# Sharing one 256-column matmul between early and late queries of a key block, in a causal attention kernel

## The chip, the core and the metric
The kernel runs on one core of a Trainium2 chip. The metric is the device time of one execution in microseconds. The core's engines are TensorE (PE, with its weight loads shown apart as PEld), VectorE (DVE), ScalarE (ACT), GpSimd (POOL) and SyncE (SP), which here only issues DMAs. Each runs its own instruction stream in order; semaphores tie them together.

## What is computed
For 64 batches of 128 tokens and 512 features, with 16 heads of 64, one shared key and value head, a learned bias, a null key and a causal mask:

```python
B, N, DIM, H, DH = (64, 128, 512, 16, 64)
xn = layernorm(x, g_in)
q = (xn @ Wq).reshape(b, n, H, DH).transpose(0, 2, 1, 3) * DH ** -0.5
kv = xn @ Wkv
k, v = kv[..., :DH], kv[..., DH:]           # then nk, nv are put in front
sim = einsum('bhid,bjd->bhij', q, k) + bias  # key 0 is the null key
sim = where(causal or masked out, -max, sim)
out = einsum('bhij,bjd->bhid', softmax(sim), v)
out = out.transpose(0, 2, 1, 3).reshape(b, n, H * DH) @ Wo
return x + layernorm(out, g_out)
```

Everything is float32. The projections (`project`, `project_out`) split each operand into a high and a low part of type fp32r and run three matmuls for one product; the scores and the product of weights and values use plain f32, for which the trace shows two weight loads and two matmul records for each call in the code.

## The kernel before
Work is tiled by batch. Two batches make a group (`GB`), two groups a pair, and `run_pairs` unrolls the first and the last of 16 pairs and loops over those between. Within a pair there are `CP` = 16 steps t, four for each batch; one step is four heads of one batch: two head pairs u, each in one half of the 128 partitions, and two heads e. Queries are split in halves: a *late* query (64 to 127) needs 128 keys, an *early* one (0 to 63) only the first 64. So a step holds 2 x 128 late logits (`BOT`) and 2 x 64 early ones (`TOP`) in each partition.

One step goes like this. PE makes the scores of two steps at once (`scores`, L387), at even t. DVE adds bias and mask and finds the largest (`logits`, L492). ACT takes the exponentials and their sums (`exponentials`, L679): late ones, then early ones. DVE inverts the sums (L501). POOL normalizes into `w_nrm` (L799, one instruction for the late, one for the early part). DVE transposes the 384 columns in blocks of 32 x 32 into `wt` (L508), which therefore has 12 blocks for each batch, 8 late and 4 early, each with 4 steps x 32 queries = 128 columns. Partition rows 32g to 32g+31 of `wt` hold the queries' block with u = g // 2 and h = g % 2, where h says which 32 of the 64 queries of a half.

Once a batch, after its four steps, PE multiplies weights and values (`values`, L411): for each g, each head e and each key block j that the queries of that block need, one call with 32 rows, 64 columns of values as weights and the 128 columns of one block of `wt` as moving data. It writes into `ps_pv[g]`, whose 256 columns are step c, late or early l, query q. h = 0 needs late blocks 0, 1, 2 and early block 0; h = 1 needs late 0 to 3 and early 0, 1. With u and e that is 16 + 24 = 40 calls. `ITEMS` is that list, and the loop takes rank r of it on all of g before the next rank. A pair (g, e) is one 32 x 64 tile of the PE array; there are eight.

Then ACT adds the null value and makes the high part (`heads_hi`, L687, four instructions, one for each g), DVE the low part (`heads_lo`, L513, four), and PE multiplies with Wo (`project_out`, L424, 24 matmuls of 512 columns). `project_out` waits for `o_lo_made` to be two, i.e. for the second of the four `heads_lo`, and after 12 matmuls for the fourth. It writes into the bank of `ps_pv[0]`. Layernorm, residual and store follow.

The order on each engine is written out by hand. On PE a step is: scores if t is even, `values` if due, parts of the next projections (`front`: x transposes L448, kv and q projections L430, 12 matmuls for each part) and `project_out` if due. By `PLAN`, `values` and the `heads` of a batch are due in the same even step and `project_out` in the one after. The first batch of a group has `values` at t % 8 = 6, followed by one q part of 12 matmuls; the second has it at t % 8 = 2, followed by the kv part of 12 matmuls. On ACT an even step is: late exponentials, the four `heads_hi`, early exponentials. On DVE it is: logits of two steps, the four `heads_lo`, then copies of q (L568) and transposes.

Of the kernel before, what the change touches and what calls it, by code (L numbers as in the profile page):

```python
# [12 lines left out]
B, N, DIM = 64, 128, 512  # L13
H, DH = 16, 64
# [14 lines left out]
HALF = N // 2  # L29
BLK = 32  # L30
BOT, TOP = 2 * N, 2 * HALF
# [33 lines left out]
STEP_STATS, STEP_XN, STEP_V, STEP_MASK = 4, 7, 7, 7  # L65


ITEMS = (
    [(1, 0), (1, 1), (1, 2), (0, 0)],
    [(1, 0), (1, 1), (1, 2), (1, 3), (0, 0), (0, 1)],  # L70
)


def attention_block(nc, x, attn_bias, null_kv, mask, g_in, null_bias, wq, wkv, wo, g_out, out):
# [4 lines left out]
    with ExitStack() as ctx:  # L79
        def sb(name, shape, dt=F32):  # L80
            return ctx.enter_context(nc.sbuf_tensor(name, shape, dt))

        def psum(name, shape):
            return ctx.enter_context(nc.psum_tensor(name, shape, F32))

        def sem(name):
            return ctx.enter_context(nc.semaphore(name))
# [43 lines left out]
        v32 = sb("v32", [P, 2, GB, N // BLK, DH])  # L131
# [8 lines left out]
        exp_bot, exp_top = sb("exp_bot", [P, 2, 2, N + 1]), sb("exp_top", [P, 2, 2, HALF + 1])  # L140
        w_sum = sb("w_sum", [P, 2, HC])
        w_inv = sb("w_inv", [P, 2, HC])
        w_nrm = sb("w_nrm", [P, 2, BOT + TOP])

        wt = sb("wt", [P, 2, WBLOCKS, CB, BLK])
# [15 lines left out]
        ps_pv = [psum(f"ps_pv{g}", [P, DIM]) for g in range(4)]  # L161
# [36 lines left out]
        pv_done, o_hi_made, o_lo_made = sem("pv_done"), sem("o_hi_made"), sem("o_lo_made")  # L198
# [18 lines left out]
        def wait(eng, s, value):  # L217

            if isinstance(value, int) and value <= 0:
                return  # L220
            eng.wait_ge(s, value)  # L221

        def apart(eng):

            eng.sem_inc(waits_taken, 1)  # L225
# [6 lines left out]

        def bot_top(row):
            return row[:, 0:BOT].rearrange("p (e n) -> p e n", e=2), row[:, BOT:].rearrange("p (e n) -> p e n", e=2)

        def steps(last):
            return range(CP + (TAIL if last else 0))
# [11 lines left out]
        def of_tile(ps):  # L249

            return ps[:, 0:2 * N].rearrange("p (c l q) -> p c l q", c=CB, l=2)
# [13 lines left out]
        block = ctx.enter_context(nc.Block())  # L265
# [105 lines left out]
        def _(pe):  # L371
# [22 lines left out]
            def values(p, batch, back):  # L394

                slot, b = back // GB % 2, back % GB
                wait(pe, wt_made, CB * batch + CB)
                wait(pe, o_lo_made, 4 * batch)
                wait(pe, y_nrm_made, batch)
                if back % GB == 0:  # L400
                    wait(pe, v_made, 2 * p + back // GB + 1)
                apart(pe)
                for r in range(len(ITEMS[1])):
                    for g in range(4):
                        if r >= len(ITEMS[g % 2]):
                            continue
                        late, j = ITEMS[g % 2][r]
                        rows = slice(BLK * g, BLK * (g + 1))
                        for e in range(2):
                            block = N // BLK * e + j if late else 2 * (N // BLK) + HALF // BLK * e + j  # L410
                            mm = pe.matmul(of_tile(ps_pv[g])[DH * e:DH * (e + 1), :, late], v32[rows, slot, b, j],  # L411
                                           wt[rows, b, block],
                                           start=(r == 0), stop=(r == len(ITEMS[g % 2]) - 1))
                            if r == len(ITEMS[g % 2]) - 1:
                                mm.then_inc(pv_done, 1)

            def project_out(batch):
                todo = [(o, w, 2 * c + u) for u in range(2) for c in range(CB)
# [45 lines left out]
            def body(p, first, last):  # L464
                for t in steps(last):
                    if t % 2 == 0 and t < CP:
                        scores(p, t)
                    for batch, back in due("pv", p, t, first, last):
                        values(p, batch, back)
                    for f, slot, kind, i in front_parts(p, t, first, last):  # L470
                        front(f, slot, kind, i)
                    if first and t == PLAN["out"]:
                        pe.wait_ge(wo_lo_by_dve, WP // 2)
                        pe.wait_ge(wo_lo_by_pool, WP // 2)
                    for batch, back in due("out", p, t, first, last):
                        project_out(batch)
# [4 lines left out]
        def _(dve):  # L481
            def logits(n, t):
                s = t % 2
                wait(dve, bias_b_made, n + 1)
                wait(dve, s_done, 2 * (n - s) + 4)
                wait(dve, exp_made, n - 1)
                apart(dve)
                for i, (bias, out_) in enumerate(zip(bot_top(bias_b[:, s]), (logit_bot[:, s], logit_top[:, s]))):
                    keys_ = bias.shape[2]
                    for e in range(2):  # L490
                        from_ = WIDE * s + N * i
                        ins = nc.vector.tensor_tensor_reduce(  # L492
                            out_[:, e, 0:keys_], ps_s[e][:, from_:from_ + keys_], bias[:, e], -1.0, 0.0,
                            ALU.add, ALU.min, neg_max[:, s, 2 * i + e:2 * i + e + 1])
                    ins.then_inc(s_read, 1)
# [285 lines left out]
        def _(pool):  # L781
            def masked_bias(n, g, t):
                slot, b, c, s = t // CG % 2, t // CB % GB, t % CB, t % 2
                if t % CG == 0:
                    wait(pool, mask_made, g + 1)
                wait(pool, s_read, 2 * (n - 1))
                for out_, bias in zip(bot_top(bias_b[:, s]), bot_top(bias_c[:, c])):
                    keys_ = out_.shape[2]
                    key_mask = mask_add[:, slot, b, 0:keys_].unsqueeze(1).to_broadcast([P, 2, keys_])
                    ins = nc.gpsimd.tensor_tensor(out_, bias, key_mask, ALU.add)  # L790
                ins.then_inc(bias_b_made, 1)

            def normalize(n, t):
                s = t % 2
                wait(pool, inv_made, n + 1)
                wait(pool, wt_made, n - 1)
                for i, (out_, w_exp) in enumerate(zip(bot_top(w_nrm[:, s]), (exp_bot, exp_top))):
                    keys_ = out_.shape[2]
                    ins = nc.gpsimd.tensor_tensor(out_, w_exp[:, s, :, 0:keys_],  # L799
                                                  w_inv[:, s, 2 * i:2 * i + 2].unsqueeze(2).to_broadcast([P, 2, keys_]),  # L800
                                                  ALU.mult)
                ins.then_inc(nrm_made, 1)
# [72 lines left out]
            def body(p, first, last):  # L875
                for t in steps(last):
                    n = CP * p + t
                    for done in due("norm", p, t, first, last):
                        y_scale(*done)
                    if t % 2 == 0 and t < CP - 2 * last:  # L880
                        for ahead in range(2, 4):
                            masked_bias(n + ahead, 2 * p + (t + ahead) // CG, (t + ahead) % CP)
                    if t < CP:
                        normalize(n, t)
                    if not last and t % CG == STEP_STATS + 1:
                        x_rstd_of(2 * p + t // CG + 2)
                    if first and t == PLAN["add"]:
                        pool.wait_ge(ld_gout, 16)
                    for done in due("add", p, t, first, last):
                        residual(*done)  # L890
                    if first and t in first_extras:
                        first_extras[t]()
# [25 lines left out]
```

## Time and profile before

| | |
|---|---|
| Time, median of three runs | 1152.41 us (1152.06, 1152.41, 1154.45) |
| Span of the profiled execution | 1154.5 us |
| PE matmul busy | 1061.4 us, 92% |
| PE weight load busy | 923.9 us, 80% |
| POOL / DVE / ACT busy | 804.2 us, 70% / 729.0 us, 63% / 674.2 us, 58% |
| Matmul records of L411 (weights x values) | 5120, 107.3 us busy |
| Matmul records of L430, xt_hi x wq_hi alone | 1024, 298.5 us busy |

The span of the profiled execution is within 0.1 us of the highest of the three times, so nothing of note lies around the span. Busy times of PE overlap each other, since the matmuls of different tiles of the array run side by side and their ends are modelled. "Busy" alone does not say that an engine sets the end; for that the chain of waits and the order in time have to be read.

### The profile page before, as it was taken

The numbers are of one execution on the slowest core, as the hardware profiler recorded it, in microseconds if no ns is written. First come the engines' busy times: TensorE is split into PE (matmuls) and PEld (weight loads), VectorE is DVE, ScalarE is ACT, GpSimd is POOL, SyncE is SP. The second block draws the span as 40 slices with busy tenths as digits, with TensorE's granted clock in tenths as the row PEclk, the third lists the DMA queues.
The fourth block names the chain that finished last, engine by engine and source line by source line (L and its number), as shares of the span: only waits on it lengthen the run. The fifth ranks groups of instructions, "written<-read, shape, count | busy, mean of one in ns | idle before, by whom it ended". The sixth has DMA issues, their size and how long they took to land.

```text
span 1154.5 us, 43028 instructions
## 1 busy us (share of the span) xinstructions
PE 1061.4 (92%) x14464; PEld 923.9 (80%) x14464; DVE 729.0 (63%) x3536; ACT 674.2 (58%) x2666; POOL 804.2 (70%) x1488
## 2 busy tenths in 40 slices
PE   4799999999999999999999999999999999999975
PEld 4678888888888888888888888888888888888864
DVE  4757666656666666766765766755766665666551
ACT  3656556566556556556655655656655656655651
POOL 2657777667777667777767777767777766777763
PEclk9999999999999999999999999999999999999987
DMA  8211211211221211220221121121121121121011
GB/s 224 64 40 49 67 57 40 66 61 45 68 65 31 67 60 47 66 67 31 65 66 44 65 66 41 55 66 56 50 68 51 45 67 58 48 66 47 30 39 36
DMA packets 51548, 67.72 MB, mean 59 GB/s; under 512 B 13888, under 2 KB 25664, under 8 KB 51392
## 3 DMA queue, kind: packets, MB, share of 16 engines
q1 hardware_dynamic: 49280, 63.21, 17.6%
q8 instruction: 138, 2.26, 0.8%
q10 hardware_dynamic: 2112, 2.10, 0.6%
q14 instruction: 18, 0.15, 0.0%
HBM read 40.11 MB, written 16.78 MB: 49 GB/s over the span
## 4 chain that ended last, share of the span: by engine, by line
PE 77%; ACT 8%; issue 6%; DVE 4%; POOL 1%; ACTq 0%; DVEq 0%; POOLq 0%
PE ps_pv L424 33%; PE ps_proj L430 32%; PE ps_s L387 7%; PE ps_pv L411 4%; ACT exp_bot L679 3%; ACT exp_top L679 2%; DVE o_lo L513 2%; ACT xt_hi L710 1%; DVE logit_bot L492 1%; PE ps_proj L448 1%; ACT o_hi L687 1%; ACTq L221 0%; DVEq L221 0%; DVE y_stats L521 0%; DVEq L225 0%
## 5 line engine op out<-in xcount | busy, mean ns | idle before, releaser
L679 ACT ACTIVATE exp_bot<-logit_bot,neg_max 128x129 f32<-128x129 f32 x512 | 201.7, 397 | 342.3 <-DVE neg_max L492 336.9
L430 PE MATMUL ps_proj<-xt_hi,wq_hi 128*128 128x256 f32 x1024 | 298.5, 292 | 4.1 <-DVE q_sb L568 3.9
L790 POOL TENSOR_TENSOR bias_b<-bias_c,mask_add 128x256 f32<-128x256 f32 (+1 forms) x512 | 289.6, 598 | 1.6 <-DVE neg_max L492 0.3
L492 DVE CUSTOM_DVE_ANT_0 logit_bot<-ps_s,bias_b 128x128 f32<-128x128 f32 x512 | 128.7, 289 | 255.4 <-PE ps_s L387 226.8
L430 PE MATMUL ps_proj<-xt_lo,wq_hi 128*128 128x256 f32 x1024 | 288.0, 281 | 0.0
L430 PE MATMUL ps_proj<-xt_hi,wq_lo 128*128 128x256 f32 x1024 | 287.9, 281 | 0.0
L424 PE MATMUL ps_pv<-wo_hi,o_hi 128*128 128x512 f32 x512 | 211.8, 414 | 51.1 <-DVE o_lo L513 51.1
L799 POOL TENSOR_TENSOR w_nrm<-exp_bot,w_inv 128x256 f32<-128x256 f32 x256 | 156.6, 612 | 120.0 <-DVE w_inv L501 118.8
L424 PE MATMUL ps_pv<-wo_lo,o_hi 128*128 128x512 f32 x512 | 204.9, 400 | 0.0
L424 PE MATMUL ps_pv<-wo_hi,o_lo 128*128 128x512 f32 x512 | 204.8, 400 | 0.0
L430 PEld LDWEIGHTS ps_proj<-xt_hi,wq_hi 128*128 128x128 f32 x1024 | 192.8, 188 | 14.3 <-issue 5.1
L430 PEld LDWEIGHTS ps_proj<-xt_hi,wq_lo 128*128 128x128 f32 x1024 | 193.0, 188 | 0.0
L430 PEld LDWEIGHTS ps_proj<-xt_lo,wq_hi 128*128 128x128 f32 x1024 | 192.9, 188 | 0.0
L679 ACT ACTIVATE exp_top<-logit_top,neg_max 128x65 f32<-128x65 f32 x512 | 172.8, 343 | 0.0
L424 PEld LDWEIGHTS ps_pv<-wo_hi,o_hi 128*128 128x128 f32 x512 | 97.7, 191 | 82.9 <-DVE o_lo L513 55.3
L508 DVE STREAM_TRANSPOSE wt<-w_nrm 128x384 f32<-128x384 f32 x256 | 131.4, 551 | 0.0
L387 PEld LDWEIGHTS ps_s<-keys,q_sb 64*64 64x64 f32 x4096 | 97.6, 133 | 39.9 <-issue 35.7
L821 POOL TENSOR_TENSOR small<-y_mv,small 128x1 f32<-128x1 f32 x64 | 12.1, 190 | 167.6 <-DVE y_mv L527 167.6
L387 PE MATMUL ps_s<-keys,q_sb 64*64 64x128 f32 (+1 forms) x4096 | 114.9, 250 | 7.2 <-DVE neg_max L492 3.7
L513 DVE SCALAR_TENSOR_TENSOR o_lo<-ps_pv,small,o_hi 128x256 fp32r<-128x256 f32 x256 | 106.2, 477 | 21.8 <-ACT o_hi L687 21.8
L424 PEld LDWEIGHTS ps_pv<-wo_hi,o_lo 128*128 128x128 f32 x512 | 97.7, 191 | 23.8
L424 PEld LDWEIGHTS ps_pv<-wo_lo,o_hi 128*128 128x128 f32 x512 | 97.9, 191 | 21.0
(61 smaller groups left out, 1850.7 us busy)
## 6 DMA issues: line engine op xcount, KB each, us to landing
x_in<-in_x_dram SPq DMA_DIRECT2D x32, 512.0 KB, 4.1
x_res<-in_x_dram SPq DMA_DIRECT2D x64, 256.0 KB, 2.8
out_dram<-y_out SPq DMA_DIRECT2D x64, 256.0 KB, 2.0
v_rep<-v_raw SPq DMA_DIRECT2D x256, 32.0 KB, 1.9
w_raw<-in_L_cond_Wq_dram ACTq DMA_DIRECT2D x4, 512.0 KB, 7.9
w_raw<-in_L_cond_Wo_dram SPq DMA_DIRECT2D x4, 512.0 KB, 6.1
mask_u<-in_mask_BxS_bk_dram SPq DMA_DIRECT2D x32, 32.0 KB, 3.7
bias_c<-in_fside_16xSxS_dram SPq DMA_DIRECT2D x4, 128.0 KB, 8.1
```

The source lines that it names most:

```text
L387: mm = pe.matmul(scored[HALF * u:HALF * (u + 1)], q_sb[rows, slot, t % CB + s, u, from_:from_ + HALF], keys[rows, slot, b, 0:N if late els ...
L411: mm = pe.matmul(of_tile(ps_pv[g])[DH * e:DH * (e + 1), :, late], v32[rows, slot, b, j], wt[rows, b, block], start=(r == 0), stop=(r == le ...
L424: mm = pe.matmul(ps_o[:], o[:, i % 2, i // 2], w[:, i], start=(j == 0), stop=(j == len(todo) - 1))
L430: mm = pe.matmul(ps[:, 0:TOK], w[:, k, cols], xt[:, k], start=(j == 0), stop=(j == len(todo) - 1))
L448: mm = pe.transpose(ps[:, N * j:N * (j + 1)], xn[:, b, P * k:P * (k + 1)], ident[:])
L492: ins = nc.vector.tensor_tensor_reduce(out_[:, e, 0:keys_], ps_s[e][:, from_:from_ + keys_], bias[:, e], -1.0, 0.0, ALU.add, ALU.min, neg_ ...
L508: nc.vector.transpose(wt[:, par, :, c], w_nrm[:, s]).then_inc(wt_made, 1)
L513: nc.vector.scalar_tensor_tensor(out=place_of(o_lo, g), in0=of_tile(ps_pv[g]), scalar=nv_col[:, 0:1], in1=place_of(o_hi, g).bitcast(F32), ...
L679: ins = nc.scalar.activation(out_[:, s, j], in_[:, s, j], ACT.Exp, bias=neg_max[:, s, k:k + 1], scale=-1.0, accum_out=w_sum[:, s, k:k + 1])
L790: ins = nc.gpsimd.tensor_tensor(out_, bias, key_mask, ALU.add)
L799: ins = nc.gpsimd.tensor_tensor(out_, w_exp[:, s, :, 0:keys_], w_inv[:, s, 2 * i:2 * i + 2].unsqueeze(2).to_broadcast([P, 2, keys_]), ALU. ...
L821: nc.gpsimd.tensor_tensor(y_var[:, c], y_mv[:, b, 1:2], eps_col[:, 0:1], ALU.add).then_inc(y_var_made, 1)
```

## The change
The list of calls in `values` becomes `VISITS`. Where both the late and the early queries of a (g, e) need key block j, one call takes the early and the late block of `wt` together, 256 columns, and writes both halves of `ps_pv[g]`. This holds for j = 0 with both h and for j = 1 with h = 1: 12 calls of 256 columns in place of 24 of 128. The 16 others keep their 128 columns. The total is 28 calls; the columns are the same 5120 for each batch. So that the early block comes first and the two blocks are a constant step apart, POOL writes the early part of `w_nrm` to the front (`top_first`) and the late one behind it; its instructions stay in the same order and size. No semaphore, wait or buffer changes.

```diff
-ITEMS = (
-    [(1, 0), (1, 1), (1, 2), (0, 0)],
-    [(1, 0), (1, 1), (1, 2), (1, 3), (0, 0), (0, 1)],
-)
+TOP_BLOCKS = TOP // BLK
+VISITS = [
+    [(0, 0, 2), (1, 0, 2)],
+    [(1, 1, 2), (0, 1, 1)],
+    [(0, 2, 1)],
+    [(1, 2, 1)],
+    [(1, 3, 1)],
+]
+KEY_BLOCKS = (3, 4)
...
+        def top_first(row):
+            return row[:, TOP:].rearrange("p (e n) -> p e n", e=2), row[:, 0:TOP].rearrange("p (e n) -> p e n", e=2)
...
-                for r in range(len(ITEMS[1])):
-                    for g in range(4):
-                        if r >= len(ITEMS[g % 2]):
-                            continue
-                        late, j = ITEMS[g % 2][r]
-                        rows = slice(BLK * g, BLK * (g + 1))
-                        for e in range(2):
-                            block = N // BLK * e + j if late else 2 * (N // BLK) + HALF // BLK * e + j
-                            mm = pe.matmul(of_tile(ps_pv[g])[DH * e:DH * (e + 1), :, late], v32[rows, slot, b, j],
-                                           wt[rows, b, block],
-                                           start=(r == 0), stop=(r == len(ITEMS[g % 2]) - 1))
-                            if r == len(ITEMS[g % 2]) - 1:
-                                mm.then_inc(pv_done, 1)
+                for visit in VISITS:
+                    for h, j, halves in visit:
+                        for u in range(2):
+                            g = 2 * u + h
+                            rows = slice(BLK * g, BLK * (g + 1))
+                            for e in range(2):
+                                top, bot = HALF // BLK * e + j, TOP_BLOCKS + N // BLK * e + j
+                                blocks = slice(top, bot + 1, bot - top) if halves == 2 else slice(bot, bot + 1)
+                                heads = of_tile(ps_pv[g])[DH * e:DH * (e + 1)].rearrange("p c l q -> p l c q")
+                                mm = pe.matmul(heads[:, 2 - halves:2], v32[rows, slot, b, j], wt[rows, b, blocks],
+                                               start=(j == 0), stop=(j == KEY_BLOCKS[h] - 1))
+                                if j == KEY_BLOCKS[h] - 1:
+                                    mm.then_inc(pv_done, 1)
...
-                for i, (out_, w_exp) in enumerate(zip(bot_top(w_nrm[:, s]), (exp_bot, exp_top))):
+                for i, (out_, w_exp) in enumerate(zip(top_first(w_nrm[:, s]), (exp_bot, exp_top))):
```

## Rows read from the trace of the kernel before

**Rows 1.** Page, parts 1 and 2: busy times; the granted PE clock in 40 slices.
```profile
PE 1061.4 (92%) x14464; PEld 923.9 (80%) x14464; DVE 729.0 (63%) x3536; ACT 674.2 (58%) x2666; POOL 804.2 (70%) x1488
...
PEclk9999999999999999999999999999999999999987
```

**Rows 2.** Page, part 4: the chain that ended last, by engine and by line.
```profile
PE 77%; ACT 8%; issue 6%; DVE 4%; POOL 1%; ACTq 0%; DVEq 0%; POOLq 0%
PE ps_pv L424 33%; PE ps_proj L430 32%; PE ps_s L387 7%; PE ps_pv L411 4%; ACT exp_bot L679 3%; ACT exp_top L679 2%; DVE o_lo L513 2%; ACT xt_hi L710 1%; DVE logit_bot L492 1%; PE ps_proj L448 1%; ACT o_hi L687 1%; ACTq L221 0%; DVEq L221 0%; DVE y_stats L521 0%; DVEq L225 0%
```

**Rows 3.** The chain in order of time, first batch of a group: start, length, what.
```profile
606.41 0.83 PE ps_s L387 x32
607.24 1.57 PE ps_pv L411 x79
608.81 1.61 PE ps_proj L430 x12
610.42 5.79 PE ps_pv L424 x24
```

**Rows 4.** Matmul records of L411 begun by 607.24, by 608.13, by 608.55.
```profile
L411 PE MATMUL ps_pv<-wt,v x8: 318/318/318, 607.2 to 607.2; 32*64 32x128 f32 x8
...
L411 PE MATMUL ps_pv<-wt,v x64: 267/268/318, 607.2 to 608.1; 32*64 32x128 f32 x64
...
L411 PE MATMUL ps_pv<-wt,v x80: 267/268/318, 607.2 to 608.5; 32*64 32x128 f32 x80
```

**Rows 5.** Timeline of PE from 609.9: start, us, engine, line, operation.
```profile
610.02 0.28 PE L430 MATMUL ps_proj<-xt_hi,wq_lo 128*128 128x256 f32 x1
610.14 0.28 PE L430 MATMUL ps_proj<-xt_lo,wq_hi 128*128 128x256 f32 x1
610.33 0.50 PE L424 MATMUL ps_pv<-wo_hi,o_hi 128*128 128x512 f32 x1
610.67 0.40 PE L424 MATMUL ps_pv<-wo_lo,o_hi 128*128 128x512 f32 x1
610.90 0.40 PE L424 MATMUL ps_pv<-wo_hi,o_lo 128*128 128x512 f32 x1
```

**Rows 6.** Second heads_lo and first weight load of L424, first batch, then second.
```profile
609.80 0.47 DVE L513 SCALAR_TENSOR_TENSOR o_lo<-ps_pv,small,o_hi 128x256 fp32r<-128x256 f32 x1
...
610.33 0.19 PEld L424 LDWEIGHTS ps_pv<-wo_hi,o_hi 128*128 128x128 f32 x1
...
627.63 0.47 DVE L513 SCALAR_TENSOR_TENSOR o_lo<-ps_pv,small,o_hi 128x256 fp32r<-128x256 f32 x1
...
628.16 0.19 PEld L424 LDWEIGHTS ps_pv<-wo_hi,o_hi 128*128 128x128 f32 x1 [1.67 <-DVE o_lo L513]
```

**Rows 7.** Timeline of DVE and ACT after the scores of 606.34, first batch.
```profile
607.57 0.29 DVE L492 CUSTOM_DVE_ANT_0 logit_bot<-ps_s,bias_b 128x128 f32<-128x128 f32 x1 [0.39 <-PE ps_s L387]
...
608.12 0.41 ACT L679 ACTIVATE exp_bot<-logit_bot,neg_max 128x129 f32<-128x129 f32 x1 [1.81 <-DVE neg_max L492]
...
608.81 0.19 ACT L679 ACTIVATION_READ_ACCUMULATOR exp_bot<-logit_bot,neg_max 128x1 f32 x1
608.90 0.47 ACT L687 ACTIVATE o_hi<-ps_pv,small 128x256 fp32r<-128x256 f32 x1
```

**Rows 8.** Another first batch, near the end: its L411, and ACT up to heads_hi.
```profile
1088.22 1.64 PE L411 MATMUL ps_pv<-wt,v 32*64 32x128 f32 x80
...
1089.90 0.19 ACT L679 ACTIVATION_READ_ACCUMULATOR exp_bot<-logit_bot,neg_max 128x1 f32 x1
1090.00 0.45 ACT L687 ACTIVATE o_hi<-ps_pv,small 128x256 fp32r<-128x256 f32 x1
```

**Rows 9.** Waits of L687 and for L513 (us, times); last L411 on the chain.
```profile
  PE ps_pv L411: 2.9, 1
...
  PEld ps_pv L424: 55.3, 33
...
1134.59 2.64 PE ps_pv L411 x80
```

## The prediction, made before the changed kernel was run
> **What bounds the kernel now.** I first read the busy times: PE has 92%, no other engine more than 70%, and the granted clock is at its full level (2.4 GHz) until the last slices [rows 1]. So PE is the engine to look at. The chain of waits says the same and gives L411, the line that changes, 4% of the span [rows 2]. Divided by the 1.57 us of one batch's L411 [rows 3] that is 1154.5 x 0.04 / 1.57 = 29 batches of 64: about one of each group of two. For that one, the first batch of a group, the chain goes through PE without a break: scores, weights x values, 12 matmuls of a q part, 24 of L424 [rows 3]. Read that way, each nanosecond that L411 loses in a first batch comes off the end. The second batch of a group is another case: its L424 sits idle for 1.67 us until the second `heads_lo` of DVE (L513) is done [rows 6].
>
> The chain follows a step back to a releaser only where it sees idle time, and matmul ends are modelled. So I ask of the first batch what L424 waits for, too. `project_out` needs the second L513. It ends at 609.80 + 0.47 = 610.27, and the first weight load of L424 starts at 610.33, 0.06 us later; in the second batch it is 627.63 + 0.47 = 628.10 and 628.16, again 0.06 us, and there it certainly waits [rows 6]. PE itself shows a dent at the same place: the q matmuls start 0.12 us apart (610.02, 610.14), so the next would start at 610.26; L424's first record starts at 610.33 and lasts 0.50 instead of 0.40 us, and the second follows 0.34 us later instead of 0.23 [rows 5]. The weight load, which elsewhere runs beside the matmul before it, lies open here. The true start of that matmul is 610.67 - 0.23 = 610.44, so PE lost 610.44 - 610.26 = 0.18 us in waiting. The chain doesn't show it because the modelled end of the last q matmul, 610.14 + 0.28 = 610.42, covers it [rows 5].
>
> What does that L513 hang on? On `heads_hi` of ACT (L687), which needs `pv_done`, the end of L411, and also stands behind the late exponentials on ACT. In this batch ACT reads the last accumulator at 608.81 and begins L687 at 608.90, 0.09 us on, and the row names no wait [rows 7]. The last L411 record had started by 608.55 [rows 4]. Whether L687 followed the one or the other can be told from a batch in which they stand differently. At 1088.22 L411 starts and has the same length of 1.64 us; L687 starts at 1090.00. That is 1.78 us after the start of L411, against 608.90 - 607.17 = 1.73 here (L411's first record is the one of 607.17, 1.64 us long to its modelled end); behind the accumulator read it is 0.10 against 0.09 us [rows 7, 8]. L687 keeps its distance to the exponentials, not to L411. And the wait list has L687 waiting for L411 once in the whole run, 2.9 us, in the last batch [rows 9]. The exponentials in turn wait for the logits, and these for the scores [rows 7], which PE issues ahead of L411. So the path through a first batch is scores, logits (607.57), late exponentials (608.12), `heads_hi` (608.90), `heads_lo`, L424 (610.33). L411 and the 12 q matmuls lie beside it, 0.18 us shorter. In a second batch they are 1.67 us shorter.
>
> **The change part by part.** *Removed:* 12 of 40 calls a batch, that is 24 of 80 matmul records and as many weight loads. *Kept:* all columns. What is it worth within L411? The last 16 records, on the four h = 1 tiles only, are four passes of a tile, and start in 608.55 - 608.12 = 0.43 us: 0.11 us a pass [rows 4]. The 64 before them, eight passes on each of the eight tiles, take 0.95 us, 0.12 us a pass. A pass is bound by its 128 columns, then, and calls for other tiles run beside it; the first eight are all under way by 607.24 [rows 4]. An h = 1 tile has six calls, 12 passes; after the change it has four calls, of which two are wide: four passes of 256 and four of 128 columns, the same 12 units. From the first to the last start it is now 608.54 - 607.17 = 1.37 us [rows 4]. Without any jostling it would be 11 units of 0.109, plus 0.05 for the first (its record is 318 ns, not 268), plus 0.05 until the last tile begins: 1.30 us. So 0.07 us is there to be regained if the lighter stream of calls feeds each tile in time. For the four passes that are merged away on a tile, the fixed cost of a matmul is bounded by L430 and L424: two of 256 columns take 2 x 0.12, one of 512 takes 0.23 [rows 5], which is 0.00 to 0.01 us for each; four give 0.00 to 0.04, and I take 0.02. L411 shrinks by 0.07 + 0.02 = 0.09 us a batch, bounds 0.00 and 0.11.
>
> What of it lies on the path: nothing in first batches, where PE would only reach L424's wait 0.18 + 0.09 us early, and nothing in second ones. That L687 waits for L411 once in the whole run says that this holds at both ends of the kernel, but for the last batch [rows 9]. There, where L411 starts at 1134.59 and ACT idles for it [rows 9], the 0.09 us, or up to twice that at the lower clock of the last slices, comes off: 0.1 us in all.
>
> *New, and not in the trace:* a call whose moving data are two runs of 128 columns and whose output goes to two halves of the bank. Its lower bound is the 0.23 us for 512 columns of L424, so no cost for width; its output now is already runs of 32 columns, with others skipped, and a pass of L411 keeps 0.11 us [rows 4]. I take a wide pass at 2 x 0.109 us. The upper bound is that such a pass runs at half that rate, 0.22 us more for each of four on an h = 1 tile. No row is near that; it makes the slow rival below.
>
> *Moved:* the early part of `w_nrm` goes in front. POOL issues the same two instructions in the same order, DVE the same transpose of 384 columns; only addresses differ: zero, and none of it is a wait. The order of the calls also changes: h = 0 ends after visit 3, h = 1 goes on alone. Even if each of the five visits waited for the one before, L411 would be 2 + 2 + 1 + 1 + 1 = 7 call times of 0.22 where it has 6 now, 0.22 more minus the 0.09 gained: 0.13 us, still within the 0.18 us of slack. What hides this edit is the chain over DVE and ACT; without that cover it would cost 30 x 0.13 = 4 us. No wait is added. Semaphore counts are the same, eight a batch.
>
> The sum against the profiled execution: 1154.5 - 0.1 = 1154.4. That execution lies 0.18% above the median of the three times, 1152.41; the same step from there gives 1152.3.
>
> **The rivals.** *Faster: L411 is on the path of first batches after all.* For it: the chain, read plainly, has L411 in about 29 batches [rows 2, 3]. Against it: the 0.06 us between L513 and L424, equal in a batch that surely waits and in one that is said not to. It gives 29 x 0.09 + 0.1 = 2.7 us: 1149.7. With the upper bound of 0.11 it is 3.3 us: 1149.1. In the same direction goes a rule of the Trainium skill: TensorEngine Tiling (Array Packing), section "Performance Considerations", puts a fixed overhead of about 60 cycles on each matmul, which at 2.4 GHz would be, as an estimate from that page, 25 ns for each of the four passes merged away on a tile, 0.10 us a batch instead of my 0.02. The trace doesn't agree, since two q matmuls of 256 columns take at most 0.01 us more than one matmul of 512 [rows 5], and even so the gain would end in the same wait.
>
> *Slower: wide calls stream at half rate.* Place: the four wide passes of an h = 1 tile. Price: 4 x 0.22 - 0.09 = 0.79 us a batch. It decides once L411 has grown by 0.18 us in first batches, i.e. from some 0.07 us for each wide pass on; second batches forgive 1.67 us. It gives 30 x (0.79 - 0.18) = 18 us, and 1 or 2 us in the last two batches, where the clock is low: 1172. Against it: a call now writes strided runs and shows nothing of it. Half the extra price, 0.39 us, would be 30 x 0.17 = 5 us: 1157.7.
>
> *It doesn't do what it says:* if the 256-column calls are taken apart again, L411 is as now, and so is the time, 1152.4. That lies within the forecast.
>
> **How the numbers follow.** A measurement of this kernel tells about 0.2% from no change, 2.3 us. The likeliest case, with the last one in it, has 0.85: 1152.3, own range 1151.0 to 1153.7 (the three times before lie within 2.4 us of each other, the lower two within 0.4). Faster rival 0.09, slower rival 0.06. The range must leave out no more than 2 in 10; the main case's own range holds nearly all of its 0.85, and I widen it a little toward the faster rival: 1150.4 to 1154.0. Faster by over 0.2%: 0.09, within: 0.85, slower: 0.06.
>
> **What would show it.** In the trace after: 56 records of L411 a batch (3584 in all) over 1.28 to 1.30 us from first to last start, not 1.37; wide passes of about 0.22 us. The first q matmul behind L411 starts 0.09 us earlier relative to it. L424's first weight load still starts 0.06 us after the second L513, and the open time before it grows from 0.18 to about 0.27 us; the chain or the waits may then name DVE L513 in first batches as well. The distance from the first logits to L424 in a first batch stays 610.33 - 607.57 = 2.76 us. I am wrong if L687 moves forward with L411, so that this distance shrinks by 0.09 us (then the faster rival holds), or if L411 grows beyond 1.37 + 0.18 us (then the slower one does).

## The result

The changed kernel is slower. Its median is 1167.2 us in four runs (1166.72 to 1169.43), that of the kernel before 1153.28 us in four; the ratio is 1.0116, with a 95% interval of 1.0095 to 1.0138. The forecast was no change, 1152.3 us, with a range that ended at 1154.0. (The ratios, here and below, are taken from the record, with their intervals; the quotient of two medians differs from them by up to 0.2%.)

The first view is the page of the changed kernel: busy times, the chain by line, and two groups of the q matmuls with the idle time before them.

```profile
PE 1062.6 (91%) x12928; PEld 914.4 (78%) x12928; DVE 730.6 (63%) x3536; ACT 674.6 (58%) x2666; POOL 804.2 (69%) x1488
...
PE ps_pv L432 33%; PE ps_proj L438 31%; PE ps_s L395 7%; PE ps_pv L420 4%; ACT exp_bot L687 3%; ACT exp_top L687 2%; DVE o_lo L521 2%; ACT xt_hi L718 1%; DVE logit_bot L500 1%; ACT o_hi L695 1%; PE ps_proj L456 1%; ACTq L226 0%; DVEq L226 0%; DVE y_stats L529 0%; DVEq L230 0%
...
L438 PE MATMUL ps_proj<-xt_hi,wq_hi 128*128 128x256 f32 x1024 | 298.5, 292 | 14.7 <-issue 10.5
...
L438 PEld LDWEIGHTS ps_proj<-xt_hi,wq_lo 128*128 128x128 f32 x1024 | 193.1, 189 | 11.7 <-issue 11.7
```

Busy times and chain are those of before [rows 1, 2]; 1536 matmul records are gone, as the code says. What is new are 10.5 us ahead of q matmuls and 11.7 us ahead of their weight loads that are put down to "issue": PE waited for nothing that a semaphore shows. The list of waits has the 10.5 us in 13 pieces. This is one of them, from the timeline of PE:

```profile
171.11 0.28 PE L438 MATMUL ps_proj<-xt_lo,wq_hi 128*128 128x256 f32 x1
171.88 0.28 PE L438 MATMUL ps_proj<-xt_hi,wq_hi 128*128 128x256 f32 x1 [0.49 <-issue]
172.00 0.28 PE L438 MATMUL ps_proj<-xt_hi,wq_lo 128*128 128x256 f32 x1
```

In the middle of a run of 24 matmuls that share their waits, one comes 0.77 us after its predecessor instead of 0.12. The same happens near 240.4, 310.0, 379.7 and so on, once in each of 13 passes of PE's loop over pairs, always between the same two matmuls, for 0.5 to 1.4 us. The 13 steps, from one start to the next, sum to 14.2 us, 12.6 us more than 13 x 0.12. The span grew by 1167.6 - 1154.5 = 13.1 us. So nearly the whole loss is there, in code that the change doesn't touch.

The product itself became shorter, by about half of what was forecast. Its records in one first batch, then the time of the whole and the first q matmul behind it:

```profile
L420 PE MATMUL ps_pv<-wt,v x56: 267/289/425, 614.5 to 615.8; 32*64 32x128 f32 x32, 32*64 32x256 f32 x24
...
614.46 1.59 PE L420 MATMUL ps_pv<-wt,v 32*64 32x256 f32 x56
615.98 0.38 PE L438 MATMUL ps_proj<-xt_hi,wq_hi 128*128 128x256 f32 x1
```

From the first record to the q matmul it is 615.98 - 614.46 = 1.52 us; before it was 1.57 [rows 3]: 0.05 us less, where 0.09 was forecast. ACT and PE behind it, in the same batch:

```profile
616.10 0.19 ACT L687 ACTIVATION_READ_ACCUMULATOR exp_bot<-logit_bot,neg_max 128x1 f32 x1
616.19 0.46 ACT L695 ACTIVATE o_hi<-ps_pv,small 128x256 fp32r<-128x256 f32 x1
...
617.08 0.48 DVE L521 SCALAR_TENSOR_TENSOR o_lo<-ps_pv,small,o_hi 128x256 fp32r<-128x256 f32 x1
...
617.61 0.19 PEld L432 LDWEIGHTS ps_pv<-wo_hi,o_hi 128*128 128x128 f32 x1 [0.16 <-DVE o_lo L521]
```

`heads_hi` starts 0.09 us behind the accumulator read as before [rows 7], the first weight load of `project_out` 617.61 - 617.56 = 0.05 us behind the second `heads_lo` [rows 6], and now the profile names that wait in a first batch too. `heads_hi` is 1.73 us behind the product's start (616.19 - 614.46), as it was. From the first logits (614.86) to `project_out` it is 2.75 us, where the prediction had 2.76.

### The profile page after: what moved, and what is told of

Its sections match the earlier page's. It is cut to its first block, busy times and chain, and to the rows that moved or that the text cites. A ratio compares the mean times of both kernels' runs of the same rounds, so it can differ in the third digit from the quotient of the medians.

```text
span 1167.6 us, 39956 instructions
## 1 busy us (share of the span) xinstructions
PE 1062.6 (91%) x12928; PEld 914.4 (78%) x12928; DVE 730.6 (63%) x3536; ACT 674.6 (58%) x2666; POOL 804.2 (69%) x1488
## 4 chain that ended last, share of the span: by engine, by line
PE 76%; ACT 8%; issue 6%; DVE 4%; DVEq 0%; ACTq 0%; POOL 0%; POOLq 0%
PE ps_pv L432 33%; PE ps_proj L438 31%; PE ps_s L395 7%; PE ps_pv L420 4%; ACT exp_bot L687 3%; ACT exp_top L687 2%; DVE o_lo L521 2%; ACT xt_hi L718 1%; DVE logit_bot L500 1%; ACT o_hi L695 1%; PE ps_proj L456 1%; ACTq L226 0%; DVEq L226 0%; DVE y_stats L529 0%; DVEq L230 0%
## 5 line engine op out<-in xcount | busy, mean ns | idle before, releaser
L687 ACT ACTIVATE exp_bot<-logit_bot,neg_max 128x129 f32<-128x129 f32 x512 | 201.5, 397 | 341.7 <-DVE neg_max L500 336.3
L438 PE MATMUL ps_proj<-xt_hi,wq_hi 128*128 128x256 f32 x1024 | 298.5, 292 | 14.7 <-issue 10.5
L438 PEld LDWEIGHTS ps_proj<-xt_hi,wq_hi 128*128 128x128 f32 x1024 | 192.9, 188 | 14.2 <-issue 5.1
L438 PEld LDWEIGHTS ps_proj<-xt_hi,wq_lo 128*128 128x128 f32 x1024 | 193.1, 189 | 11.7 <-issue 11.7
L687 ACT ACTIVATE exp_top<-logit_top,neg_max 128x65 f32<-128x65 f32 x512 | 172.6, 342 | 0.0
L576 DVE COPY q_sb<-ps_proj 128x256 f32<-128x256 f32 x256 | 105.1, 420 | 17.4 <-PE ps_proj L438 14.8
```

The lines of the kernel that those rows point to most:

```text
L438: mm = pe.matmul(ps[:, 0:TOK], w[:, k, cols], xt[:, k], start=(j == 0), stop=(j == len(todo) - 1))
L576: nc.vector.tensor_copy(q_sb[:, slot, i // 2, i % 2], ps[:, 0:TOK]).then_inc(q_made, 1)
L687: ins = nc.scalar.activation(out_[:, s, j], in_[:, s, j], ACT.Exp, bias=neg_max[:, s, k:k + 1], scale=-1.0, accum_out=w_sum[:, s, k:k + 1])
```

## What the branch has to do with it

The view of one source line shows PE's loop branch, which busy times leave out: the shortest, median and longest duration of 14 in ns. First the kernel before, then the changed one.

```profile
L229 PEldq COMPARE_BRANCH  x14: 83/3445/3827, 165.1 to 1058.7; - x14
```

```profile
L234 PEldq COMPARE_BRANCH  x14: 83/3373/3852, 165.4 to 1071.2; - x14
```

Only the last, which isn't taken, is short. The 13 jumps back take PE's sequencer 3.3 to 3.9 us in either kernel; the same view has 40 to 54 ns for ACT's. PE hides them: at the branch some 17 matmuls of `project_out` stand in its queue. In the changed kernel the branch comes at 165.40, the sequencer goes on at 168.81, and the stall ends at 171.88. In both kernels the queue that loads instructions moves nine packets of 16 KB in a pass. In the changed kernel one starts at 166.36, during the branch, and the next only at 169.46, behind it.

Counted in the traces, a pass of the loop has 1867 instructions before (59 of control, 904 weight loads, 904 matmuls) and 1675 after; a call in f32 is four, one in fp32r two. The first pair, which is unrolled, runs `values` three times, so 3 x 12 x 4 = 144 instructions ahead of the loop are gone as well. From the loop's start to the stall the changed kernel has 4 of control, 16 score calls with 64, and 13 more up to the weight load of the seventh q matmul: 81.

**Theory A (code).** PE's instructions come in blocks. A jump back has the first block loaded, and the next only behind it. Where the loop starts close to the end of a block, PE runs dry before the next one is there. The change moved the loop by 144 instructions, and the wide calls have nothing to do with the loss. The Trainium skill says the like on the page Runtime: NRT & Kernel Launch, section Instruction fetch mechanics: code is fetched in blocks of 16 KiB, which are 256 instructions, and "Branching breaks sequential prefetch". **Theory B (wide calls).** Something about 256-column calls, or a shorter product, brings the stall about.

## Experiments

Loop passes below are means over the 13 from branch to branch in the profiled execution. Before: 68.73 us; changed kernel: 69.68 us. "Border at 81" means that a block ends 81 instructions behind the loop's start.

**1. 56 and 24 instructions more ahead of the loop, changed kernel.**

```diff
+            for _ in range(56):          # 24 in the second kernel
+                pe.sem_inc(padding, 1)
             pe.wait_ge(ident_made, 1)
             for kind, i in PROLOGUE:
```

> The changed kernel with 56 semaphore increments put at the very start of PE's program, where PE idles for the first x anyway. In the changed kernel PE stands still once in each of 13 loop passes, 0.5 to 1.4 us, 14 us in all, always behind the 7th q matmul after the loop's branch. Code theory: what stalls is the supply of PE's instructions behind the branch; it depends on where the loop's start lies in the stream, and 56 instructions more ahead of the loop move that. Then the 13 stalls go and the time is that of the kernel before, 1151.5 to 1154. Wide-call theory: 256-column calls cost PE something that is paid later in the pass; the padding changes nothing, 1166 to 1169. The Trainium skill, page Runtime: NRT & Kernel Launch, section Instruction fetch mechanics, says that code comes in blocks of 256 instructions and that a taken branch breaks the sequential prefetch; no row shows the block size yet.

> The changed kernel with 24 increments at the start of PE's program. Code theory, with a block border that the stall shows some 49 instructions behind the loop's start: the border comes 24 instructions earlier, in the 11th or so of the 16 score calls, 23 x 2 - 24 instructions in; PE runs dry earlier by the work of 5 score calls and 7 q matmuls, some 1.1 us, while the code arrives at the same time. So 13 stalls of 1.6 to 2.5 us inside L395, and 1178 to 1184 us. Wide-call theory: stalls stay where they are, 1166 to 1169 us.

Measured: 1194.01 us with 56, ratio 1.0344 (1.0327 to 1.0361); 1191.2 us with 24, ratio 1.0301 (1.0275 to 1.0326). Passes of 71.73 and 71.70 us. The stall moved into the scores. With 24, then with 56:

```profile
166.40 0.88 PE L396 MATMUL ps_s<-keys,q_sb 64*64 64x128 f32 x26
168.88 0.34 PE L396 MATMUL ps_s<-keys,q_sb 64*64 64x64 f32 x6 [1.60 <-issue]
```

```profile
166.38 0.65 PE L396 MATMUL ps_s<-keys,q_sb 64*64 64x128 f32 x10
169.03 0.71 PE L396 MATMUL ps_s<-keys,q_sb 64*64 64x128 f32 x11 [2.00 <-issue]
```

Of the 32 score records 26 and 10 come ahead of the gap. By weight loads, which the trace has complete, the gap lies behind the 27th and the 11th. At two instructions a record that is 53 and 21 behind the four of control, against 77 in the changed kernel: 24 and 56 less, to the instruction. So the place of the stall is fixed to how many instructions lie ahead of the loop. Theory B, by which padding changes nothing, fails here. My first forecast, that 56 would cure it, failed too: I had taken a score call for two instructions, not four, and so held 56 for enough to push the border out of the front of the loop. The cost was also larger than the 1178 to 1184 us expected with 24: the stall itself is about 1.8 us, the pass 3.0 us longer than before. The last 1.2 us go with TensorE's clock. Five of the 13 passes with 24 take 70.2 to 71.0 us, which is the pass of before and the stall. In each of the eight others, of 72.2 to 72.7 us, the granted clock is at its lower level (1.2 GHz) for 3.4 us, and the matmuls of a q part start 0.21 us apart instead of 0.12; such a pass takes 1.9 us more than the others in the mean, and 8 x 1.9 / 13 = 1.2. In the second pass no matmul starts between 237.8 and 239.7, and the clock is down from 240.8; the third column from the end is the granted clock:

```profile
240.90:244.10 3.20, 3.20 (x17) 3.20 (x16) 2.15 (x15) 1.53 (x8) 0.94 (x3) 0.50 0.46 166
```

With 56 this happens in seven passes of 13. In the loops of the kernel before and of the changed kernel it happens in none.

**2. The kernel before with 184 instructions more.** The same edit, with 184, in the kernel before.

> The kernel before, all 40 calls of 128 columns, with 184 semaphore increments put at the start of PE's program. The changed kernel has 36 calls less ahead of the loop (3 batches x 12); at two instructions for a call that is 72, and 184 more would be the same place modulo 256. Code theory: the kernel before gets the stalls of the changed one, one in each of 13 passes, some 0.5 to 1.4 us each, behind about the 7th q matmul after the branch, and 1164 to 1169 us. Wide-call theory: no stall, 1152 to 1154 us.

Measured: 1218.3 us, ratio 1.0553 (1.0531 to 1.0575), far above the 1164 to 1169 us expected. Passes take 72.09 us, again with the clock at its lower level for 3.4 us in six of them, and the first branch comes 17.7 us later, which is the increments themselves: each takes PE 0.15 us, and only some 70 of them fit into its idle start of 11 us. 13 x 3.36 + 17.7 = 61.4 us, and the span grew by 1215.8 - 1154.5 = 61.3. The gap came, but at another place than expected:

```profile
187.08 0.40 PE L388 MATMUL ps_s<-keys,q_sb 64*64 64x128 f32 x2
189.90 0.69 PE L388 MATMUL ps_s<-keys,q_sb 64*64 64x128 f32 x16 [2.42 <-issue]
```

It lies behind the third weight load, 5 + 4 = 9 instructions from the loop's start. That measures the block: the kernel before has 144 more ahead of the loop than the changed one, so its border is at 81 - 144, and 184 more bring it to 81 - 328 = -247. That -247 and 9 are the same place takes a block of 256. The kernel before itself then has its border at 81 - 144 + 256 = 193. That is behind the first scores, 36 matmuls of q parts and the x transposes, among the scores of t = 2, and PE gets there some 11 us after the branch begins. In the four kernels with stalls so far the stall ends 6.2 to 7.3 us after the branch begins, whether the border is at 81, 57, 25 or 9. So in the kernel before the next block is there in time.

**3. The kernel before with its border at 81.**

```diff
+            for _ in range(64):
+                pe.sem_inc(padding, 1)
             pe.wait_ge(ident_made, 1)
...
                     for batch, back in due("out", p, t, first, last):
                         project_out(batch)
+                        if first:
+                            for _ in range(16):
+                                pe.sem_inc(padding, 1)
```

> The kernel before, 40 calls of 128 columns, with 112 increments ahead of the loop: 64 at the start, 16 behind each of the first three project_out. By the count (before: border at 193 from the loop's start) this puts the border at 81, where the changed kernel has it. Code theory: branches of 3.3 to 3.9 us, a stall of 0.5 to 1.4 us behind the 7th q matmul in each of 13 passes, passes of 69.1 to 70.1 us, 10 to 16 us more than before, ratio 1.009 to 1.014, with not one wide call. Wide-call theory: ratio 0.999 to 1.003.

Measured: 1170.07 us, ratio 1.0108 (1.0086 to 1.0129), next to the changed kernel's 1.0116; passes of 69.83 us. With 40 calls of 128 columns and no wide one the stall is at the same matmul, the seventh of the q part:

```profile
171.20 0.28 PE L431 MATMUL ps_proj<-xt_lo,wq_hi 128*128 128x256 f32 x1
172.46 0.28 PE L431 MATMUL ps_proj<-xt_hi,wq_hi 128*128 128x256 f32 x1 [0.98 <-issue]
```

This is the whole loss of the change, made without the change. The stall ends 6.2 to 7.3 us after the branch begins, here too.

**4. The changed kernel with its border at 240.** As in 3, with 64 increments and 11 in place of 16.

> The changed kernel with 97 semaphore increments ahead of PE's loop: 64 at the start, 11 behind each of the first three project_out, where PE has some 16 matmuls queued and the increments cost nothing. Code theory, now in blocks of 256 instructions: counted from the loop's start, a block border stood at 81 in the changed kernel (the stall), and goes to 81 - 97 + 256 = 240. The loop's 1675 instructions then touch 7 blocks, not 8. In the kernel with 144 increments and 16 calls the loop touched 7 as well, its branches took 0.21 us, not 3.3 to 3.9, and nothing was fetched in the loop. So here too: branches of 0.2 us, no stall, passes of 68.7 us as in the kernel before, ratio 0.997 to 1.001. Wide-call theory: ratio still 1.01. Theory that the branch fetch itself cost something in the kernel before: 13 x 0.03 us less.

Measured: 1155.99 us against 1155.56, ratio 0.9998 (0.9985 to 1.0011); passes of 68.69 us. So this is the change without its side effect (and with the loop kept, as the branch shows): nothing that can be measured in the time. The branch now:

```profile
L235 PEldq COMPARE_BRANCH  x14: 76/208/238, 163.4 to 1056.5; - x14
```

And the DMA queues between 200 and 1000 us, first in the kernel before, then here:

```profile
q1 hardware_dynamic: 32313, 44.04, 17.4%
q8 instruction: 105, 1.72, 0.9%
```

```profile
## 3 DMA queue, kind: packets, MB, share of 16 engines
q1 hardware_dynamic: 32352, 44.06, 17.5%
issues: line engine op xcount, KB each, median us to landing
```

The instruction queue is gone: the loop stays on the engine. Its 1675 instructions touch 1 + 6 blocks with the border at 240, and 1 + 7 with it at 81 ((1675 - 81) / 256 = 6.2). All kernels here with seven blocks have short branches and no loading in the loop, all with eight or more have long ones; the kernel of 2, whose loop touches nine, loads ten packets a pass. The kernel of 5 has its border at 81, as the changed kernel has, but seven blocks, and no stall: a border close behind the loop's start costs only where the loop isn't kept. The page of the Trainium skill named above gives PE's instruction memory as 2048 instructions, eight blocks; that a loop of eight isn't kept while one of seven is would fit one block being held for what comes next, which no run shows. That page of the Trainium skill also speaks of a target outside the current two pages; for PE the runs differ, as seven blocks were kept. Compared with the kernel before, keeping the loop and the change together gave 68.73 - 68.69 = 0.04 us a pass: PE's queue had hidden the 3.4 us already.

**5. Less of the product.** Sixteen calls a batch in the kernel before, for key block 0 alone; the calls for blocks 1 to 3 are left out.

```diff
 ITEMS = (
-    [(1, 0), (1, 1), (1, 2), (0, 0)],
-    [(1, 0), (1, 1), (1, 2), (1, 3), (0, 0), (0, 1)],
+    [(1, 0), (0, 0)],
+    [(1, 0), (0, 0)],
 )
```

with 144 increments at the start.

> The kernel before with 16 of the 40 calls of each batch: key block 0 alone, late and early, for all (g, e); the calls for key blocks 1 to 3 are left out. 144 increments at PE's start stand for the 72 calls that are missing ahead of the loop. It takes some 0.9 us from weights x values in each batch. Theory of the prediction, that the product hangs beside the DVE and ACT chain and that L424 waits for the second heads_lo in every batch: nothing is gained but in the last batch, 1150.5 to 1153.5 us, with the first weight load of L424 0.05 us behind the second L513. Rival, the chain as the page prints it, with the product on the path of 29 batches: 29 x 0.9 = 26 us less, 1127 us.

Measured: 1174.71 us, ratio 1.0164 (1.0137 to 1.019). The time isn't the test here: the first branch comes 13.3 us later than before, 11.5 of them for increments ahead of PE's first matmul, more than I had allowed for. The passes are, and ten of 13 take 68.66 to 68.69 us, with the product some 0.9 us shorter in each of four batches (its records start within 0.43 us, not 1.37). The waits in one pass, from 247.1 to 315.8 us (total, times, longest):

```profile
PEld ps_pv L425 <- DVE o_lo L516: 6.2, 4, 2.0
```

All four batches of the pass wait for `heads_lo`, and nothing is gained. The other three passes take 70.2 us. In each of them PE's granted clock is at the lower level of 1.2 GHz for 3.4 us. In the first it is down from 436.4, 1.4 us after PE had idled for 2.1 us; the third column from the end is 0.50 here:

```profile
436.57:439.55 2.98, 2.98 (x8) 2.34 (x7) 0.34 (x3) 2.08 (x10) 2.52 (x4) 0.50 0.00 0
```

**6. More of the product.** In the changed kernel at 240, one more wide call on each h = 1 tile, then two. Early queries get blocks there that they shouldn't.

```diff
-    [(1, 2, 1)],
-    [(1, 3, 1)],
+    [(1, 2, 2)],
+    [(1, 3, 2)],          # stays (1, 3, 1) in the smaller step
```

> As the changed kernel with its border at 240, but the calls for key blocks 2 and 3 of h = 1 are made wide too (the early half gets blocks that it should not, so the output changes). No instruction more: four passes of an h = 1 tile take 0.22 us in place of 0.11, L420 grows by 0.44 us in each batch. Theory of the prediction: the product has a slack in first batches, 0.18 us before plus the 0.05 us that the change took, 0.23; the rest, 0.2 us, is paid in 30 or 31 first batches and nothing in second ones: 6 to 7 us more than the kernel with the border at 240, passes of 68.7 + 2 x 0.2 = 69.1 us. Rival, product on the path of the first batches, as the chain says: 0.44 x 2 = 0.9 us a pass, 13 us. Rival, in all four: 1.8 us a pass, 28 us.

> As the changed kernel at border 240, but only the call for key block 2 of h = 1 is made wide too (the early half gets a block that it should not). L420 ends 0.22 us later, its last pass is narrow as in the changed kernel. It measures how much later the product may end before heads_hi on ACT waits for it. Theory of the prediction, slack 0.18 + 0.05 us set by PE: nothing is paid, passes of 68.7 us. Theory after the kernel with two such calls, where L701 waited for L421 and each first batch paid 0.41 us: the slack is that of heads_hi on ACT, between 0.05 us (what the change took off) and 0.1 us: 0.12 to 0.17 us for each first batch, passes of 68.93 to 69.03 us. If there is no slack at all: 69.13.

Measured: with two, 1171.56 us, ratio 1.0118 (1.009 to 1.0147), passes of 69.51 us, 0.82 more than in 4; with one, passes of 69.10 us, 0.41 more (a single run, 1161.94 us). Second batches pay nothing, so each first batch pays 0.41 and 0.20 us. That is all that the product grew by: in the trace its last pass ends 0.39 us later with two, and its last record starts 0.18 us later with one. Who waits is seen on ACT with two wide calls (the kernel of 4 has this wait once, 2.7 us, in the last batch):

```profile
  PE ps_pv L421: 13.2, 33
...
406.82 0.18 ACT L693 ACTIVATION_READ_ACCUMULATOR exp_bot<-logit_bot,neg_max 128x1 f32 x1
407.31 0.48 ACT L701 ACTIVATE o_hi<-ps_pv,small 128x256 fp32r<-128x256 f32 x1 [0.30 <-PE ps_pv L421]
```

`heads_hi` had been 0.09 us behind the accumulator read; it is 0.49 now and waits for the product. With one wide call it is 0.27. There, and in the kernel of 4, where `heads_hi` waits for nothing, one batch each reads:

```profile
403.46 0.47 ACT L701 ACTIVATE o_hi<-ps_pv,small 128x256 fp32r<-128x256 f32 x1
...
400.81 0.45 ACT L701 ACTIVATE o_hi<-ps_pv,small 128x256 fp32r<-128x256 f32 x1
```

The product's last record starts at 403.05 and at 400.40, 0.41 us ahead in both, and so it is in 24 first batches of either kernel, to 0.01 us. So in the changed kernel nothing is left of the slack: a shorter product gains nothing, and a longer one costs from the first nanosecond. In the kernel before, `heads_hi` starts 0.36 us behind the last record and doesn't wait, so 0.41 isn't the least distance there; how much slack that kernel had these runs don't tell.

**7. Filling the idle time ahead of `project_out`.** Twelve q matmuls are moved to the step in which PE waits.

```diff
-    4: [("q", 0, 1), ("q", 1, 1)],
+    3: [("q", 0, 1)],
+    4: [("q", 1, 1)],
```

> As the changed kernel with its border at 240, but the 12 matmuls of the next group's first q part are issued at t % 8 = 3, ahead of project_out, instead of at t % 8 = 4. In second batches PE idles 1.7 us there for the second heads_lo. If the theory holds that L424 waits for that in every batch, 1.41 us of that idle time is filled 31 times and the pass drops by up to 2.8 us: 65.9 to 66.8 us, 1110 to 1125 us in all, unless DVE's copy of q or the scores behind it become the next wait. If instead PE alone sets the pace by its work, no change, 1150 to 1155.

> The kernel before, 40 calls, no increments added, only the q part moved: 12 matmuls at t % 8 = 3 ahead of project_out instead of at t % 8 = 4. With the changed kernel at border 240 this move gave passes of 67.13 us and a ratio of 0.977. If that gain is the idle time ahead of L424 alone, it owes nothing to the wide calls or to resident code: passes of 67.1 to 67.3 us, ratio 0.975 to 0.980. If it needs the shorter product or a loop that isn't fetched anew, passes of 67.6 us and more, ratio above 0.982.

Measured: 1130.64 us on top of the kernel of 4, ratio 0.9768 (0.9748 to 0.9789), and 1131.93 us on top of the kernel before, ratio 0.9794 (0.976 to 0.9829); passes of 67.13 us in both. This beats both kernels by some 2%, though the second interval reaches down to 1.7%, and it owes nothing to the wide calls or to where the loop lies. The gain is 1.56 us a pass, little over half of the 2.8 that was its upper bound. The wait ahead of `project_out` in a second and then a first batch of the first of these kernels:

```profile
411.03 0.19 PEld L434 LDWEIGHTS ps_pv<-wo_hi,o_hi 128*128 128x128 f32 x1 [0.26 <-DVE o_lo L528]
```

```profile
393.20 0.19 PEld L434 LDWEIGHTS ps_pv<-wo_hi,o_hi 128*128 128x128 f32 x1 [0.80 <-DVE o_lo L528]
```

Second batches idle 0.26 us, not 1.67 [rows 6], but first ones 0.80, where they had been nearly tight. Their chain of waits now comes from POOL:

```profile
421.94 1.57 POOL bias_b L805 x3
423.51 0.43 POOL w_nrm L814
424.03 0.41 POOL w_nrm L814
...
425.36 0.45 ACT o_hi L702
```

**8. The same for first batches.** Q part 5 goes from t % 8 = 0 to 7, on top of 7.

```diff
-    0: [("q", 5, 0), ("q", 6, 0)],
+    0: [("q", 6, 0)],
+    7: [("q", 5, 1)],
```

> As the kernel with the early q part (passes of 67.13 us), and the 12 matmuls of q part 5 moved from the next group's t = 0 to t = 7, ahead of project_out of the first batch, where PE now idles 0.75 us for the second heads_lo. If PE's idle time there is all that is left, up to 0.75 us of it is filled in two batches of a pass: 65.6 to 66.4 us, ratio 0.955 to 0.967. If the chain over the mask bias and the normalization on POOL and the exponentials sets the first batch, as the chain of waits of that kernel says, L424 starts later by what the part takes beyond the gap and nothing is gained, or something lost: 67.0 to 68.0 us.

Measured: 1131.64 us, ratio 0.9792 (0.9757 to 0.9828), passes of 67.23 us. Nothing gained, a tenth of a microsecond a pass lost (67.23 - 67.13): as that chain says, PE's idle time there is no longer what sets the pace.

## Why the prediction was wrong

**What bounds the kernel** held. `project_out` waits for the second `heads_lo` in every batch, 0.05 us behind it, though the chain had the product in 4% of the span; taking 0.9 us off the product in every batch gained nothing (5). The chain's share of a line was no price for it.

**The product's gain** held in kind and was smaller: 0.05 us a batch, not 0.09 (bounds 0.00 and 0.11). With the stalls gone the change is worth 0.9998 (4), which is the forecast "no change". Two slips of the working don't bear on that. The half-priced slower case takes 0.17 us from 0.35 - 0.18 but names the growth 0.39. And the 1154.5 us of the profiled execution were read as the 1154.45 us of the list, while in the runs recorded later the time is 1.8 us or more above the span (1169.43 against 1167.6 in the changed kernel).

**"What hides this edit", the 0.18 us of slack, failed.** I took it from PE's gap ahead of L424, which is the slack on only one of the two ways by which the product reaches that gap. On the other, `pv_done` to `heads_hi` on ACT, I argued that `heads_hi` doesn't wait, but not by how much. In the changed kernel that way is tight: 0.20 us were paid for 0.18 more (6). A call with more work in it would have cost there, where I wrote that up to 0.18 us would be free. This error didn't make the miss, since the product became shorter.

**The step that made the error is the list of what the change removes.** It counted 24 matmul records a batch and gave them a price on PE's array, and a price of zero elsewhere. They are also code. 144 instructions fewer ahead of the loop moved its start against the blocks of 256, from a border at 193 to one at 81 (192 fewer in the loop itself left it at eight blocks), and PE stood still 13 times, with 0.5 to 1.4 us between two matmuls: some 12.6 of the 13.1 us lost. Shown by moving the border alone, both ways: the kernel before with its border at 81 is 1.0108, the changed one with its border at 240, where its loop is also kept, is 0.9998. Not one of my rivals had it; the slower one, wide calls at half rate, gave 1172 and so came near the result for a reason that isn't there (the wide pass is no slower, 1.52 us for the product).

It could have been seen as a risk: the branch of 3.4 us and nine packets of code a pass are in the trace of the kernel before. How close the border was couldn't be read from it: all places of borders here are counted from a stall that a run showed.

## What to carry to other kernels

Where a loop runs on PE and its branch takes microseconds in the trace, every edit to the program also moves the loop's start; before a change of 1% is put down to what was edited, look for a gap behind the branch that no semaphore explains, count from it to the loop's start, and move the loop with padding, in both directions. A line's share in the chain is a price only if the wait behind it moves with it: compare the distance from the supposed releaser over batches, on each way that leads there. Slack has to be taken on the tightest of these ways. And a stall can cost more than its length, where the clock falls behind it.

## What the runs showed of the hardware

PE's instructions came in blocks of 256: with 24, 56, 112 and 184 instructions more ahead of the loop the gap stood where a border at multiples of 256 puts it. A loop of PE that touched seven blocks was kept and its branch took 0.21 us; with eight or more it took 3.3 to 3.9 us and all its code was loaded anew in each pass. After such a jump that landed with 9 to 81 instructions left in its block, 0.5 to 2.9 us passed between two matmuls, although PE's queue had hidden the jump itself; PE went on 6.2 to 7.3 us after the branch began. In the three kernels with the longest stalls (1 and 2: 1.4 to 2.9 us between two matmuls) the granted clock fell to 0.50, the lower level, for 3.4 us in 21 of 39 passes, within 1.6 us of the stall's end, and such passes took 1.3 to 1.9 us longer in the mean than the others. The page Advanced Engine Details and Errata of the Trainium skill, section Control Flow Timing, gives about 108 ns for a compare and branch; the traces have 76 to 83 ns for one not taken and 207 to 243 ns for one within kept code.
